# Attention and expert layer on one core: query-key products as 64-row, 64-column matmuls, two heads at a time

## What is computed

```python
attn_scores = jnp.einsum('bihd,bjhd->bhij', q, k) / scale
logits = li[:, :, None, :] + lj[:, None, :, :] + rel_b          # three relation logits for each pair i, j
relation_probs = jax.nn.softmax(logits, axis=-1)
bias = jnp.einsum('bijk,hk->bhij', relation_probs, logical_bias)
attn_scores = attn_scores + gate * bias
attn_weights = jax.nn.softmax(attn_scores, axis=-1)
out = jnp.einsum('bhij,bjhd->bihd', attn_weights, v)
```

## Time and profile before

| what | us |
|---|---|
| median of 3 runs | 5007.06 (5003.76 to 5009.56) |
| the profiled execution's own time | 5018.32 |
| its span, first to last instruction | 5016.4 |
| TensorE matmuls busy | 4458.2 (89%) |
| VectorE busy | 3821.7 (76%) |
| ScalarE busy | 3380.7 (67%) |
| GpSimd busy | 2057.0 (41%) |

### The profile page before, as it was taken

One profiled execution on the slowest core, in us unless ns is written; L12 is line 12 of the kernel. 1 busy time (PEld: TensorE's weight loads), 2 busy tenths in 40 slices (PEclk: granted clock), 3 DMA queues, 4 the chain that ended last, 5 costly groups with the idle time before them and its releaser, 6 DMA issues. The chain is left out here.

```text
span 5016.4 us, 183232 instructions
## 1 busy us (share of the span) xinstructions
PE 4458.2 (89%) x74128; PEld 3458.1 (69%) x74128; DVE 3821.7 (76%) x6309; ACT 3380.7 (67%) x4458; POOL 2057.0 (41%) x1809
## 2 busy tenths in 40 slices
PE   6459999999999999999999999999999996289992
PEld 3227777777777777777777777777777785267771
DVE  4388888888888888888888888888888843167773
ACT  2017887888787788877877787888888882044440
POOL 0114444444444444444444444444444442433335
PEclk9659999999999999999999999999999998589996
DMA  7514544544555445554454455454554456244434
GB/s 96 82 33 112 118 113 111 118 112 115 113 112 112 111 114 116 113 118 110 114 114 112 109 113 116 113 119 115 115 114 111 112 114 178 79 146 149 150 137 113
DMA packets 496919, 573.65 MB, mean 114 GB/s; under 512 B 136360, under 2 KB 369704, under 8 KB 492096
## 3 DMA queue, kind: packets, MB, share of 16 engines
q1 hardware_dynamic: 486880, 543.96, 46.5%
q0 software_dynamic: 6144, 16.79, 1.1%
q10 hardware_dynamic: 3040, 0.98, 0.1%
HBM read 305.10 MB, written 46.65 MB: 70 GB/s over the span
## 5 line engine op out<-in xcount | busy, mean ns | idle before, releaser
L734 DVE TENSOR_REDUCE b_mxp<-b_mx 128x1 f32<-128x512 f32 x4096 | 2635.4, 686 | 559.0 <-PE b_mx L835 508.9
L703 ACT ACTIVATE b_pr<-b_sc 128x1024 f32<-128x1024 f32 x2048 | 1986.5, 1021 | 697.0 <-PE b_sc L824 689.2
L814 PE MATMUL b_sc<-b_qm,kst 128*128 128x128 f16 x16384 | 1272.3, 220 | 54.3 <-ACT b_pr L703 42.0
L824 PE MATMUL b_sc<-b_cm,b_rst 112*128 112x128 f16 x16384 | 1264.5, 220 | 42.8 <-DMA b_rst<-b_rhi 35.5
L814 PEld LDWEIGHTS b_sc<-b_qm,kst 128*128 128x128 f16 x16384 | 971.6, 98 | 283.7 <-issue 229.5
L860 PE MATMUL b_acc<-b_pr,vp 128*32 128x128 f32 x32768 | 1124.1, 277 | 27.3 <-issue 26.9
L824 PEld LDWEIGHTS b_sc<-b_cm,b_rst 112*128 112x128 f16 x16384 | 1012.0, 98 | 49.4 <-DMA b_rst<-b_rhi 40.4
L860 PEld LDWEIGHTS b_acc<-b_pr,vp 128*32 128x32 f32 x32768 | 839.2, 110 | 265.2 <-ACT b_pr L703 190.2
L636 POOL TENSOR_TENSOR b_ex<-b_ex 128x512 f32<-128x512 f32 x512 | 654.7, 1279 | 680.8 <-ACT b_ex L682 680.8
L835 PE MATMUL b_mx<-kst,b_qx 64*128 64x512 f16 x4096 | 819.4, 397 | 92.1 <-DVE b_mxp L734 76.9
L642 POOL CAST b_rhi<-b_ex 128x512 f16<-128x512 f32 x512 | 312.8, 611 | 1293.0 <-ACT b_ex L690 1244.5
(11 more groups left out here) (144 smaller groups left out, 1726.0 us busy)
## 6 DMA issues: line engine op xcount, KB each, us to landing
b_dj<-key_logits SPq DMA_DIRECT2D x256, 768.0 KB, 7.9
b_rst<-b_rhi SPq DMA_DIRECT2D x2048, 64.0 KB, 3.2
b_rst<-b_rlo SPq DMA_DIRECT2D x1024, 64.0 KB, 3.1
c_w1r<-in_L_ffn_W_dram SPq DMA_DIRECT2D x23, 1024.0 KB, 4.9
c_w2r<-in_L_ffn_W_dram SPq DMA_DIRECT2D x23, 1024.0 KB, 4.8
expert_tokens<-c_zeros SPq DMA_DIRECT2D x23, 512.0 KB, 6.8
c_xb<-expert_tokens SPq DMA_DIRECT2D x23, 512.0 KB
expert_results<-c_y SPq DMA_DIRECT2D x23, 512.0 KB, 2.9
```

The source lines that it names most:

```text
L703: nc.scalar.activation(pr[:, jt % 2, half, :], sc[:, half].rearrange("p a b -> p (a b)"), ACT.Exp).then_inc(s["p_ready"], 1)
L734: nc.vector.tensor_reduce(mxp[:, head, part:part + 1], mx[:, (bank + ab) % MX_RING, :], AX.X, ALU.max).then_inc(s["mx_used"], 1)
L814: pe.matmul(sc[:, half, side, p * P:p * P + P], kst[:, pair, jt * P:jt * P + P], qm[:, par, :, pair, side * IS:side * IS + IS], start=(p = ...
L824: ins = pe.matmul(out, rst[:, u % 2, b, j0:j0 + P], cm[:, par, half, b], start=False, stop=(b % (NB // 2) == NB // 2 - 1), skip_group_chec ...
```

## The change

The products become matmuls of 64 rows (one head) and 64 columns (64 queries of that head), 32 a step in place of 16, issued alternately for the lower and the upper 64 rows, with outputs in different banks. The halves of `sc` are now even and odd heads. All 16 relation matmuls of a step come first (and open the accumulation), the 32 products last; `scores_ready` counts both halves at the end of the products. `pe_pv` waits once, for both exponentials. The tokens' layout changes so that the eight blocks of a chunk are adjacent, and `sp_r` needs 3 DMAs for each k, of twice the size. `sp_q`, `sp_qx`, `sp_m_out` and `sp_m_in` move on SP's queue; the two loads of `const[:, :, 0:4]` become one.

```diff
 def by_block(tokens):
-    return tokens.rearrange("o (t s i b) d -> (o s) b i t d", s=2, i=BI, b=NB // 2)
+    return tokens.rearrange("o (t i b) d -> (o b) i t d", i=BI, b=NB)
...
-            for side in range(2):
-                sp.dma_start(const[IS * side:IS * side + IS, par, 0:4],
-                             const_dram[bass.ds(x, 1)].rearrange("o (s b i) n -> (o s) i b n", s=2, b=NB // 2)[side, :, :, 0:4]
-                             ).then_inc(s[f"const_in{par}"], 16)
+            sp.dma_start(const[:, par, 0:4],
+                         const_dram[bass.ds(x, 1)].rearrange("o (b i) n -> (o i) b n", b=NB)[:, :, 0:4]).then_inc(s[f"const_in{par}"], 16)
...
-            for side in range(2):
-                for part, t in enumerate((rhi, rlo, rhi)):
-                    row = 32 * part + BI * k
-                    sp.dma_start(rst[row:row + BI, u % 2, NB // 2 * side:NB // 2 * side + NB // 2, :],
-                                 t[IS * side:IS * side + IS, 2 * (u % 2) + k, :]).then_inc(s[f"r_in{u % 2}"], 16)
+            for part, t in enumerate((rhi, rlo, rhi)):
+                row = 32 * part + BI * k
+                sp.dma_start(rst[row:row + BI, u % 2], t[:, 2 * (u % 2) + k, :]).then_inc(s[f"r_in{u % 2}"], 16)
...
-                        if u == 0 and k == 0 and not last:
-                            sp_q(sp, c + 1, 1 - par)
-                        if u == M_UNIT and not last:
-                            if k == 0:
-                                sp_m_out(sp, c + 1)
-                            else:
-                                sp_m_in(sp, c + 1, 1 - par)
                     if u + 4 < UNITS or not last:
                         sp.wait_ge(s["d_ready"], 32 * c + 4 * u + 12)
                         waited(sp)
                         sp_dj(sp, (u + 4) % UNITS)
                     if u == 1:
                         sp_att(sp, c)
-                        if more:
-                            sp.wait_ge(s["c_made"], 2 * c + 2)
-                            waited(sp)
-                            sp_qx(sp, c + 2, par)
+                    if u == 2 and not last:
+                        sp_q(sp, c + 1, 1 - par)
+                    if u == 3 and more:
+                        sp.wait_ge(s["c_made"], 2 * c + 2)
+                        waited(sp)
+                        sp_qx(sp, c + 2, par)
+                    if u == M_UNIT and not last:
+                        sp_m_out(sp, c + 1)
+                        sp_m_in(sp, c + 1, 1 - par)
...
+        def pe_relation(pe, c, par, jt, half):
+            u, j0 = jt // 4, jt % 4 * P
+            if jt == 0:
+                pe.wait_ge(s["c_made"], 2 * c + half + 1)
+            if jt % 4 == 0 and half == 0:
+                pe.wait_ge(s[f"r_in{u % 2}"], 96 * (UNITS // 2 * c + u // 2 + 1))
+            if not (isinstance(c, int) and c == 0 and jt == 0):
+                pe.wait_ge(s["p_ready"], STEPS * c + 2 * jt + half - 1)
+            for b in range(NB):
+                side, i0 = b // (NB // 2), b % (NB // 2) * BI
+                out = sc[:, half, side, :].rearrange("p (h i) -> p h i", h=HH)[:, :, i0:i0 + BI]
+                pe.matmul(out, rst[:, u % 2, b, j0:j0 + P], cm[:, par, half, b], start=(i0 == 0), stop=False,
+                          skip_group_check=True)
+
+        def pe_products(pe, c, par, jt):
+            if jt == 0:
+                pe.wait_ge(s["q_in"], 64 * c + 64)
+            for pair in range(PAIRS):
+                for side in range(2):
+                    for ab in range(2):
+                        rows = slice(64 * ab, 64 * ab + 64)
+                        ins = pe.matmul(sc[:, ab, side, pair * IS:pair * IS + IS], kst[rows, pair, jt * P:jt * P + P],
+                                        qm[rows, par, ab, pair, side * IS:side * IS + IS], start=False,
+                                        stop=(pair == PAIRS - 1), skip_group_check=True)
+                        if pair == PAIRS - 1 and side == 1:
+                            ins.then_inc(s["scores_ready"], 1)
+
+        def pe_scores(pe, c, par, jt):
+            for half in range(2):
+                pe_relation(pe, c, par, jt, half)
+            pe_products(pe, c, par, jt)
...
-            for half in range(2):
-                pe.wait_ge(s["p_ready"], STEPS * c + 2 * jt + half + 1)
-                for k in range(HH):
-                    h = HH * half + k
-                    ins = pe.matmul(acc[32 * (h % 4):32 * (h % 4) + 32, h // 4, :], vp[:, jt, VW * h:VW * h + 32],
-                                    pr[:, jt % 2, half].rearrange("p (a h i) -> p h a i", a=2, h=HH)[:, k],
-                                    start=(jt == 0 and half == 0 and k < 4), stop=(jt == NT - 1), skip_group_check=True)
+            pe.wait_ge(s["p_ready"], STEPS * c + 2 * jt + 2)
+            for h in range(H):
+                ins = pe.matmul(acc[32 * (h % 4):32 * (h % 4) + 32, h // 4, :], vp[:, jt, VW * h:VW * h + 32],
+                                pr[:, jt % 2, h % 2].rearrange("p (a h i) -> p h a i", a=2, h=HH)[:, h // 2],
+                                start=(jt == 0 and h < 4), stop=(jt == NT - 1), skip_group_check=True)
```

More of the change, by code:

```diff
@@ L190, in _ @@
                     sp.dma_start(x[BI * b:BI * b + BI, 8 * q:8 * q + 8, :],
-                                 by_block(hidden)[b // 4, b % 4, :, 8 * q:8 * q + 8, :]).then_inc(x_in[q], 16)
+                                 by_block(hidden)[b, :, 8 * q:8 * q + 8, :]).then_inc(x_in[q], 16)
             for m in (2, 3, 0, 1):
@@ L626, in pool_c @@
             nc.gpsimd.tensor_tensor(cm[:, par, half],
-                                    cval[:, par, :, HH * half:HH * half + HH].unsqueeze(3).broadcast_to([ROWS, NB, HH, BI]),
+                                    cval[:, par, :, half:H:2].unsqueeze(3).broadcast_to([ROWS, NB, HH, BI]),
                                     eye[:, :].unsqueeze(1).unsqueeze(1).broadcast_to([ROWS, NB, HH, BI]),
@@ L638, in pool_r @@
             if not (isinstance(x, int) and x == 0 and u < 2):
-                pool.wait_ge(s[f"r_in{u % 2}"], 192 * (UNITS // 2 * x + u // 2))
+                pool.wait_ge(s[f"r_in{u % 2}"], 96 * (UNITS // 2 * x + u // 2))
             pool.sem_inc(s["pool_waited"], 1)
@@ L717, in dve_d @@
             if g == 0 and n == 0:
-                dve.wait_ge(s[f"const_in{par}"], 48 * nth)
+                dve.wait_ge(s[f"const_in{par}"], 32 * nth)
             if k == 0 and n == 0:
@@ L801, in _ @@
             dve_out(dve, NT)
-        def pe_scores(pe, c, par, jt, half):
+        def pe_relation(pe, c, par, jt, half):
             u, j0 = jt // 4, jt % 4 * P
-            if jt == 0 and half == 0:
-                pe.wait_ge(s["q_in"], 64 * c + 64)
-            if not (isinstance(c, int) and c == 0 and jt == 0):
-                pe.wait_ge(s["p_ready"], STEPS * c + 2 * jt + half - 1)
-            for p in range(4):
-                pair = 4 * half + p
-                for side in range(2):
-                    pe.matmul(sc[:, half, side, p * P:p * P + P], kst[:, pair, jt * P:jt * P + P],
-                              qm[:, par, :, pair, side * IS:side * IS + IS], start=(p == 0), stop=False,
-                              skip_group_check=True)
             if jt == 0:
@@ L819, in pe_scores @@
             if jt % 4 == 0 and half == 0:
-                pe.wait_ge(s[f"r_in{u % 2}"], 192 * (UNITS // 2 * c + u // 2 + 1))
+                pe.wait_ge(s[f"r_in{u % 2}"], 96 * (UNITS // 2 * c + u // 2 + 1))
+            if not (isinstance(c, int) and c == 0 and jt == 0):
+                pe.wait_ge(s["p_ready"], STEPS * c + 2 * jt + half - 1)
             for b in range(NB):
@@ L823, in pe_scores @@
                 out = sc[:, half, side, :].rearrange("p (h i) -> p h i", h=HH)[:, :, i0:i0 + BI]
-                ins = pe.matmul(out, rst[:, u % 2, b, j0:j0 + P], cm[:, par, half, b], start=False,
-                                stop=(b % (NB // 2) == NB // 2 - 1), skip_group_check=True)
-            ins.then_inc(s["scores_ready"], 1)
+                pe.matmul(out, rst[:, u % 2, b, j0:j0 + P], cm[:, par, half, b], start=(i0 == 0), stop=False,
[16 more added lines that the diff above has]
+            pe_products(pe, c, par, jt)
         def pe_pair(pe, x, par, nth, n, bank):
@@ L881, in _ @@
             pe.wait_ge(s["ones_made"], 1)
-            for half in range(2):
-                pe_scores(pe, 0, 0, 0, half)
+            pe_scores(pe, 0, 0, 0)
             def chunk(c, par, nth, last):
@@ L888, in chunk @@
                     if jt < NT - 1:
-                        for half in range(2):
-                            pe_scores(pe, c, par, jt + 1, half)
+                        pe_scores(pe, c, par, jt + 1)
                     elif not last:
-                        for half in range(2):
-                            pe_scores(pe, c + 1, 1 - par, 0, half)
+                        pe_scores(pe, c + 1, 1 - par, 0)
                     pe_step_pair(pe, c, par, nth, jt, 0, last, more)
@@ L1050, in _ @@
```

(4 more changed lines are left out.)

## The result

The changed kernel takes 5555.6 us (median of 4 runs, 5522.94 to 5566.23), the kernel before 5005.41 (5000.68 to 5009.56). The ratio is 1.1089, 95% interval 1.1039 to 1.1138: 11% slower, where 6% faster was forecast. The profiled execution took 5547.69 us.

The account below looks back on a forecast made before the run. TensorE was taken to set the step of 3.55 us. From the profiled 5018.3 us, -368 - 39 + 40 + 12 + 20 = -335 gave 4683, 4672 against the runs' median, stated as 4685 with unfound waits; range 4620 to 4900.

Parts of the forecast that it names:

- Parts 1 and 2: Products and step length: 32 small products take 0.46 us, the step falls from 3.55 to 3.19, saving 368 us.
- X: Time of a step's 32 small products on TensorE: 0.46 us taken, with 0.43 as lower bound.
- Loads not hidden: Rival on the products: each row half loads and streams in turn, step 3.37 us, 4870 us in all; chance 0.19.
- The queue sets the pace: Rival on the products: TensorE's queue needs 27 ns per load and matmul, 5105 us in all; chance 0.15.
- The change doesn't do what it says: Rival on the products: the two row halves don't overlap at all, 6050 us in all; chance 0.03.
- The loop through ScalarE: Step length: exponentials start behind the last product, half 1's relation matmuls wait for the second exponential; 3.19 us.
- TensorE's sum: Step length if TensorE's own work alone set it: 1.65 + 0.85 + 0.15 + 0.47 = 3.12 us.
- Part 3: Copies of rst, six a unit: the waits for them, 39 us over the whole, taken as gone.
- Part 4: Row bounds, once a chunk: TensorE loses 2.25 us instead of 1.0, +40 us at 32 chunks.
- about 1.9 for L556 to land (L562's value): Row bounds: landing time assumed for the L556 copy behind the dj load, about 1.9 us.
- The bounds come later still: Rival on the row bounds: 3 us more per chunk, 4785 us in all; chance 0.06.
- Part 5: Small terms: issue stalls grow by a quarter with the instruction rate, +12 us; waits that had cover, +20 us.

Follow-up runs that it names:

- e7_both: Changed kernel with the row-bounds copies ahead of unit 6's dj load and each dj load in three of 256 KB: 5046.20 us, 1.009 of before.
- e5_bounds_first: Changed kernel with the two row-bounds copies ahead of unit 6's dj load instead of behind it: 5362.11 us, 1.0715 of before.
- e10_dj_twice: Kernel before with each dj load issued a second time, into a tile that nothing reads: 6164.61 us, 1.2316 of before.
- e3_split: Kernel before with each product split into two of 128 rows and 64 columns, 168 TensorE instructions a step: 5210.25 us, 1.0391 of before.
- e6_split_dj: Changed kernel with each 768 KB dj load in three of 256 KB, about a step apart, bounds still behind: 5254.84 us, 1.0501 of before.

## Why the prediction was wrong

**Parts 1 and 2 were right.** X, put at 0.46 us, is 0.48; the step, put at 3.19, is 3.22. The 340 us saved stand against 368 forecast. The two row halves do work side by side: 32 products in 0.48 us is 15 ns from start to start. So *Loads not hidden* (X = 0.64), *The queue sets the pace* (0.87, with a turning point at 24 ns a product) and *The change doesn't do what it says* (1.79) all fall, and the 25 ns that the Trainium skill, "TensorE: Matmul & The Clock Gate", section Wait — 56ns, not 53.3ns?, gives as the least distance does not hold across row halves here. The loop through ScalarE, which set 3.19, is seen in the changed kernel's trace: in an undisturbed step the first relation matmul of half 1 starts 0.143 us after the one before it, where 0.056 is the distance of the others, and 0.055 after the end of the second exponential (medians). Without this wait of 0.09 the step would be 3.13 us, TensorE's sum (3.12 forecast). One count in part 1 holds only for the old order, half by half: with all products ahead of all relation matmuls there would be four changes of kind too, not six. No term hangs on it.

**Part 3 was right for its row** and not for its neighbours: matmuls' waits for `rst` fell from 32.9 to 11.1 us. The `qm` and `qx` loads, which I took as needed late and so free where they stand, cost as soon as the queue is full: in e7_both, 164 us of waits for `rst`.

**Part 4 was mis-sized: +40 us forecast, some 150 measured.** The 193 us that e5_bounds_first gives back are all that the late bounds cost; about 32 of them (1.0 us a chunk, by part 4) the kernel before paid too. Over the whole attention TensorE's waits for ScalarE rose by 145 us. What was mis-sized was "about 1.9 for L556 to land (L562's value)". I took the landing time of a small copy with no large load just ahead of it. (The parts as named there also add up to 6.75 us, not 6.9, which changes nothing.) Issued directly behind 768 KB it is 6.8 us in the changed kernel; with the copies ahead of the load 2.8. The median issue to landing, of the kernel after and of e5_bounds_first:

```profile
row_bounds<-b_m SPq DMA_DIRECT2D x26, 4.0 KB, 6.8
```

```profile
row_bounds<-b_m SPq DMA_DIRECT2D x28, 4.0 KB, 2.8
```

The rival *The bounds come later still* had the mechanism: 3 us more per chunk where 5.8 were measured (12.7 us from bound to GpSimd for the 6.9 forecast), and with part 4's own 40 a price of 140 us, which is about what was measured.

**Part 5 is the step that failed: +12 us for issue stalls, +394 measured on TensorE in the middle 3650 us, +451 over the whole attention.** I saw that the rate goes from 38 to 53 instructions per us, above the highest that the trace had held for 100 us, and scaled the old stalls by the rate. But these stalls are not proportional: they are what is left when a hole in the supply is longer than what TensorE has in hand. The hole (few fetches start for 4 us behind each `dj` load) was in the trace of before, at no cost except 50 us, and so were its two signs that I did not look up: the fetches as a queue of their own, and their times against the loads. Three runs show the parts of it apart: the load alone makes the stalls (e10_dj_twice, 609 us at the old rate), the rate alone makes them (e3_split, 165 us with the old load), and pieces of the load take them away (e6_split_dj, 60 us at the new rate). My one test for the supply, the rate of the rival *The queue sets the pace*, was about a load and a matmul in TensorE's queue, in steady running; what failed was how instructions get to it.

To the stalls comes the clock. The busy times and the granted clock (third number from the end) before, in and behind the stop, in the changed kernel:

```profile
2041.00:2043.50 2.50, 2.50 (x68) 1.84 (x71) 2.25 (x5) 2.37 (x4) 0.41 (x1) 1.00 0.56 157
2044.00:2047.00 3.00, 0.19 (x7) 0.00 (x0) 0.51 (x1) 1.98 (x4) 1.89 (x2) 0.98 0.86 112
2048.00:2050.00 2.00, 2.00 (x26) 1.80 (x26) 1.68 (x3) 0.00 (x0) 0.00 (x0) 0.50 0.64 87
```

After TensorE stood from 2044 to 2047 it got 0.50, its lower level of 1.2 GHz, where it had 1.00, the upper; at that level the 16 relation matmuls cost 0.73 us more. In the whole attention the lower level was granted for 768 us in 143 stretches, each with a stop of TensorE shortly ahead of it; before it was 55 us in 15. To price it I took each run of matmuls of one kind, idle time left out, against the median of its kind at the upper level: 275 us, before 25. The clock was in no term of the sum.

With it the loss adds up, over the whole attention: -340 for the regular steps, +451 issue (501.8 against 51.1), +145 waits for ScalarE (186.8 against 42.0), +28 for VectorE, -19 for `rst`, +250 clock make 515 us, of 526. The two causes carry most of it, since without both (e7_both) the kernel is 509 us faster; of that the clock, which costs 111 us there, is a good part. *Why* a fetch doesn't start while a load is under way, no row shows. The Trainium skill, "DMA: Bandwidth & Descriptors", section Queues, rings and completion order, says that each DMA engine takes its queues in turn, a whole packet of descriptors from one before it goes to the next. With 384 descriptors of 2 KB in a load (768 KB by the 2 KB of the rows above), 24 for each of the 16 DMA engines, that rule would fit a hole as long as a load and its shortening by pieces of 8 each, if the 24 went as one packet; the page calls 9 to 17 descriptors typical. No run varied the descriptors at one size, so this stays an argument.

What the profile of the changed kernel was to show came out so: products of about 190 ns, exponentials close behind the last product, and `rst` waits all but gone; of the signs that I named for being wrong, the last, issue stalls more than doubled, came true: they are nine times those of before.

## What to carry to other kernels

Before raising the number of small TensorE instructions per microsecond, look at the queue of instruction fetches against the large loads: if fetches pause behind a load, work out how long the pause is and what the new rate uses up in it. Cut large broadcast loads into pieces with work between them, and put small copies that an engine waits for ahead of them, never directly behind. Time a transfer by where it will stand in the queue, not by a row in which no large load stood ahead of it. And price a stop of TensorE with what follows it: here 250 us of slower work at the lower clock came with some 600 us more of idle time.

## What was not expected of the hardware

- Products of 64 rows and 64 columns, alternating between the lower and upper rows, start 15 ns apart (32 in 0.48 us), with a weight load each.
- Instruction fetches of 16 KB almost stop behind a 768 KB load: 6 fetches in the 1 to 5 us behind 210 loads, 189 in the 5 to 8 us; with two such loads in a row the pause is 10 us. TensorE goes on some 1.5 us after the fetch has landed, and its stops lie a multiple of 256 instructions apart (178 of 181).
- Half of the value matmuls, on two of four strips of 32 partitions, take TensorE as long as all of them on four (0.80 and 0.81 us from first to last start).
- A 4 KB copy directly behind a 768 KB load of the same queue lands after 6.8 us instead of 1.4.
- An added load of 768 KB per unit whose data nothing reads, though VectorE waits for its landing, cost 1159 us (5006 to 6165), over a fifth of the kernel, with no instruction added on TensorE.
